# Three stages of a four-layer conv network: merged gates and moved projections in a state-space scan, re-ordered passes in an edge stage, four buffers and two queues for the norm statistics

## The reference, cut to what matters

```python
def _gn(v, G=16, eps=1e-5):
    B_, C_, H_, W_ = v.shape
    g = v.reshape(B_, G, C_ // G, H_, W_)
    m = jnp.mean(g, axis=(2, 3, 4), keepdims=True)
    s = jnp.var(g, axis=(2, 3, 4), keepdims=True)
    return ((g - m) / jnp.sqrt(s + eps)).reshape(v.shape)
...
x = x + L0(_gn(x)); x = x + L1(_gn(x)); x = x + L2(_gn(x)); x = x + L3(x's edge operators and an hourglass)
```

```python
xi, z = jnp.split(xz_, 2, axis=-1)
xi = jax.nn.silu(causal_dwconv1d(xi.transpose(0, 2, 1), conv1d_w, conv1d_b)).transpose(0, 2, 1)
x_dbl = xi @ x_proj_w.T
dt = jax.nn.softplus(x_dbl[..., :DT_RANK] @ dt_proj_w.T + dt_proj_b)
Bm = x_dbl[..., DT_RANK:DT_RANK + D_STATE]
Cm = x_dbl[..., DT_RANK + D_STATE:]
dA = jnp.exp(dt[..., None] * A); dBu = dt[..., None] * Bm[:, :, None, :] * u[..., None]   # in selective_scan
h = scan of h = dA * h + dBu along the sequence
y = jnp.einsum('bldn,bln->bld', h, Cm) + u * D          # u is xi
return y * jax.nn.silu(z)                               # then out_proj
```

## Time and profile before

| | us |
|---|---|
| median of 3 runs | 18979.34 (18858.6 to 18991.37) |
| the profiled run, its own time | 18992.29 |
| span of that run in the trace | 18990.6 |

### The profile page before, as it was taken

One profiled execution on the slowest core, in us unless ns is written; L12 is line 12 of the kernel. 1 busy time (PEld: TensorE's weight loads), 2 busy tenths in 40 slices (PEclk: granted clock), 3 DMA queues, 4 the chain that ended last, 5 costly groups with the idle time before them and its releaser, 6 DMA issues. The chain is left out here.

```text
span 18990.6 us, 422049 instructions
## 1 busy us (share of the span) xinstructions
PE 15091.1 (79%) x162396; PEld 5743.9 (30%) x162396; DVE 14262.7 (75%) x12961; ACT 12928.0 (68%) x20898; POOL 9582.0 (50%) x8230
## 2 busy tenths in 40 slices
PE   5888888888885668888888888848888886658877
PEld 2333333333332312222222222212222222435554
...
GB/s 80 12 11 12 11 12 11 12 11 12 11 12 103 112 53 16 17 17 17 17 17 17 17 17 17 15 100 32 43 35 37 42 33 59 166 48 32 32 46 132
DMA packets 773987, 711.83 MB, mean 37 GB/s; under 512 B 260672, under 2 KB 671456, under 8 KB 753384
## 3 DMA queue, kind: packets, MB, share of 16 engines
q1 hardware_dynamic: 691736, 584.15, 11.8%
...
...
## 5 line engine op out<-in xcount | busy, mean ns | idle before, releaser
L270 DVE TENSOR_TENSOR l_mx<-l_p_v,l_puN 128x2048 f32<-128x2048 f32 x2560 | 5636.4, 2278 | 154.9 <-PE l_p_s L485 142.2
L485 PE MATMUL l_p_s<-l_mx,l_w2z 128*32 128x512 f32 x32768 | 3825.9, 611 | 588.7 <-ACT l_mx L397 319.6
L290 POOL TENSOR_TENSOR l_mx<-l_pv,l_puP 128x2048 f32<-128x2048 f32 x1024 | 3716.7, 3646 | 319.3 <-PE l_p_s L485 313.5
L1270 POOL TENSOR_TENSOR l1m_hc<-l1m_hs,l1m_cs 128x512 f32<-128x512 f32 x2304 | 2929.1, 1271 | 8.5 <-DVE l1m_hs L1222 8.1
L1222 DVE TENSOR_TENSOR_SCAN l1m_hs<-l1m_da,l1m_carry,l1m_pu 128x512 f32<-128x512 f32 x2304 | 2823.5, 1267 | 106.2 <-ACT l1m_da L1140 2.2
L416 ACT ACTIVATE l_mx<-l_pv,l_puP 128x128 f32<-128x128 f32 x8192 | 2446.9, 393 | 0.8
L1212 DVE TENSOR_TENSOR l1m_pu<-l1m_pu,l1m_bs 128x512 f32<-128x512 f32 x2304 | 1475.8, 686 | 1102.2 <-PE l1m_pu L975 1102.2
L397 ACT ACTIVATE l_mx<-l_mx 128x2048 f32<-128x2048 f32 x1024 | 1954.5, 1909 | 46.3 <-POOL l_mx L290 46.0
L485 PEld LDWEIGHTS l_p_s<-l_mx,l_w2z 128*32 128x32 f32 x32768 | 983.4, 112 | 3029.3 <-issue 1770.0
L1140 ACT ACTIVATE l1m_da<-l1m_pr,l1m_an 128x512 f32<-128x512 f32 x2304 | 1459.0, 684 | 565.3 <-PE l1m_pr L968 414.6
L975 PE MATMUL l1m_pu<-l1m_dts,l1m_sl 32*128 32x512 f32 x4608 | 1415.9, 690 | 480.4 <-ACT l1m_da L1140 470.7
...
## 6 DMA issues: line engine op xcount, KB each, us to landing
...
l_xs<-in_x_dram SPq DMA_DIRECT2D x128, 256.0 KB, 3.0
x_after<-l_ot SPq DMA_DIRECT2D x128, 256.0 KB, 2.4
...
```

The costliest lines, as they stand in the source:

```text
L270: v.tensor_tensor(mx[:, r % QB, :, :, :], columns.unsqueeze(1).broadcast_to([P, 4, G, P]), rows.broadcast_to([P, 4, G, P]), ALU.max).then_ ...
L290: g.tensor_tensor(mx[:, r % QB, :, :, :], pv[:, u, :, :].unsqueeze(1).broadcast_to([P, 4, G, P]), rows.broadcast_to([P, 4, G, P]), ALU.add ...
L485: ins = pe.matmul(p_s[R * q:R * (q + 1), 512 * u:512 * (u + 1)], w2z[:, 31 - r:63 - r], mx[:, r % QB, q, :, :].rearrange("p t v -> p (t v) ...
L1270: g.tensor_tensor(hc[:, (3 * u + p) % 6, part, :], hs[:, p % 3, part, :], cs[:, u, :], ALU.mult).then_inc(hc_done, 1)
```

## The change

**norm_table.** `xt` has four buffers. The even images are loaded by SP, the odd ones by ACT's queue; a load of image n waits until the statistics of image n-4 are done. The loops are unrolled.

**state_space.** The uses of `pp` stand in the order X0, X1, DT0, DT1, BB, CC, Z0, Z1, OUT. ACT no longer applies Silu to PSUM: drain_x (p = 0, 1) and drain_z (p = 7, 8) write a half into a new SBUF tile `raw`, and both gates are applied in p = 2, two halves in one instruction each (gate_x for chunk n, gate_z for chunk i), with a table load before and an explicit one behind. The matmuls follow the drains: x_proj(n,1) at p = 1, z_proj at p = 7 and 8. dt_proj waits for gate_x, POOL's gate for gate_z. DVE's multiplication of a pair is one instruction over two banks, and the skip of the chunk behind stands ahead of pair 2's multiplication.

**edges.** POOL clears the whole of `xs` in one memset (14256 columns) in place of its four borders; the gathers stand ahead of passes(0); in the loop weigh(b+1) is first and all seven early passes of image b+2 follow pool(b,0). `sides` and `rim` are rewritten, with the same matmuls in the same order.

```diff
-        xt = m.sb("xt", [P, 2, N])
+        xt = m.sb("xt", [P, 4, N])
...
-                    sp.wait_ge(s_free, j * 2 + u + 1)
-                    sp.dma_start(xt[:, u, :], image[at(j * 2 + u), :, :].rearrange("b p n -> p (b n)")).then_inc(s_load[u], 16)
+            for n in range(0, B, 2):
+                if n >= 4:
+                    sp.wait_ge(s_free, n - 1)
+                sp.dma_start(xt[:, n % 4, :], image[n]).then_inc(s_load[n % 4], 16)
...
         @block.scalar
         def _(act):
+            for n in range(1, B, 2):
+                if n >= 4:
+                    act.wait_ge(s_free, n - 1)
+                act.dma_start(xt[:, n % 4, :], image[n]).then_inc(s_load[n % 4], 16)
...
-    X0, Z0, X1, Z1, DT0, DT1, BB, CC, OUT = range(USES)
+    X0, X1, DT0, DT1, BB, CC, Z0, Z1, OUT = range(USES)
...
             def dt_proj(n, un, ho):
+                pe.wait_ge(xi_ready, n + 1)
                 into_pp(n, (DT0, DT1)[ho])
...
                     if p == 1 and not last:
-                        z_proj(n, un, 0)
-                    if p == 2 and not last:
                         x_proj(n, un, 1)
-                        z_proj(n, un, 1)
...
+                        if p == 7:
+                            z_proj(n, un, 0)
+                        if p == 8:
+                            z_proj(n, un, 1)
                     if p == 8:
                         out_proj(i, use_of(N, 0) if last else use_of(n, OUT))
...
-                act.activation(xi[:, un, hf, :], pp[:, :], ACT.Silu, bias=cols[:, 0, hf:hf + 1]).then_inc(pp_drained, 1)
+                act.activation(raw[:, 0, hf, :], pp[:, :], ACT.Identity, bias=cols[:, 0, hf:hf + 1]).then_inc(pp_drained, 1)
...
-                act.activation(sz[:, un, hf, :], pp[:, :], ACT.Silu).then_inc(pp_drained, 1)
+                act.activation(raw[:, 1, hf, :], pp[:, :], ACT.Copy).then_inc(pp_drained, uses)
+
+            def gate_x(n, un, ahead):
+
+                act.wait_ge(pp_drained, use_of(n, X1) + 1)
+                if ahead:
+                    act.wait_ge(y1_done, n * 2)
+                act.activation(xi[:, un], raw[:, 0], ACT.Silu).then_inc(xi_ready, 1)
+
+            def gate_z(i, u):
+
+                act.wait_ge(pp_drained, use_of(i, Z1) + 1)
+                act.wait_ge(y2_done, i * 2 + 1)
+                act.activation(sz[:, u], raw[:, 1], ACT.Silu).then_inc(sz_ready, 1)
...
+                    if p == 2:
+                        if not last:
+                            a_of(n, un, jn)
+                            gate_x(n, un, True)
+                        gate_z(i, u)
+                        act.preload_act_table_set("natural_log_exp_and_others")
                     if not last:
                         if p == 0:
-                            gate_x(n, un, 0, True)
+                            drain_x(n, 0, True)
                         if p == 1:
-                            gate_z(n, un, 0, True)
-                        if p == 2:
-                            a_of(n, un, jn)
-                            gate_x(n, un, 1, True)
-                            gate_z(n, un, 1, True)
+                            drain_x(n, 1, True)
...
+                        if p == 7:
+                            drain_z(n, 0, True)
+                        if p == 8:
+                            drain_z(n, 1, True)
                     if p == 8:
                         out_copy(j, u, use_of(N, 0) if last else use_of(n, OUT))
...
-                for part in range(2):
-                    bank = 2 * ((u + p) % 2) + part
-                    tile = pu[:, LC * bank:LC * (bank + 1)]
-                    dve.tensor_tensor(tile, tile, bs[:, u, :], ALU.mult).then_inc(dbu_done, 1)
+                bank = 2 * ((u + p) % 2)
+                tile = pu[:, LC * bank:LC * (bank + 2)].rearrange("p (a n) -> p a n", a=2)
+                dve.tensor_tensor(tile, tile, bs[:, u, :].unsqueeze(1).broadcast_to([NB, 2, LC]), ALU.mult).then_inc(dbu_done, 2)
...
                 for p in range(PAIRS):
+                    if p == 2:
+                        skip(i - 1, 1 - u, 1, i * D_IN + (8 + 4))
                     inputs_by_b(i, u, p)
                     scans(i, u, p)
-                    if p == 2:
-                        skip(i - 1, 1 - u, 1, i * D_IN + (8 + 4))
...
-            g.memset(xs[:, :, :, 0:2], 0.0)
-            g.memset(xs[:, :, :, W + 2:W + 4], 0.0)
-            g.memset(xs[:, :, 0:2, 2:W + 2], 0.0)
-            g.memset(xs[:, :, XR - 2:XR, 2:W + 2], 0.0).then_inc(zeroed, 1)
+            g.memset(xs[:], 0.0).then_inc(zeroed, 1)
...
             for b in range(B):
-                if b + 2 < B:
-                    passes(b + 2, 0, 2)
                 if b + 1 < B:
                     weigh(b + 1)
                 pool(b, 0)
                 if b + 2 < B:
-                    passes(b + 2, 2, 7)
+                    passes(b + 2, 0, 7)
```

204 lines of the change are left out of this document (99 added, 105 removed).

## The result

The changed kernel took 18184.19 us (median of 4, 18156.89 to 18191.61), the kernel before 18918.97 beside it: a ratio of 0.9609, with an interval from 0.956 to 0.9657. The forecast was 18050, its wide range 17850 to 18430, the likeliest case's own range 17960 to 18200. The profiled run spans 18189.9 us against 18990.6, 800.7 less; the forecast gain was 935.

A forecast was written before the change was run, and what follows sets the result against it. The prediction took DVE, with holes in it, to bound the state-space stage. From 18992 it subtracted 755 (state space), 64 (statistics) and 116 (edges), giving 18057, predicted as 18050; likeliest range 17960 to 18200, wide range 17850 to 18430.

The forecast's parts named there:

- the likeliest case: Whole kernel: state-space chunk near 37.6 us, time 18050 us, own range 17960 to 18200, chance 0.44.
- the wait at pair 5: State-space stage: DVE loses 1.0 us at full clock or 1.9 at 1.2 GHz, behind both loads and gates.
- most of it at pair 5: State-space sign of being right: DVE waits about 3 us per chunk, mostly at pair 5 and ahead of the skip.
- The cover of the edge stage: Edge stage: the 16.23 us wait ahead of pool(b,1) has room for the two moved passes, 9.3 us.
- the first step of the chain: State-space chunk: replicate(0) starts about 2.2 us after DVE's first multiplication, behind the second z_proj and out_proj's drain.
- a sign of being wrong: State-space stage: replicate(0) starting later than 2.2 us into the chunk would show the prediction wrong.
- The rest of the chain: State-space chunk after replicate(0): PE and ACT steps bring replicate(4) at 19.6 us; later projections are covered by DVE's pairs.
- 0.8 for the skip: State-space stage: DVE loses about 0.8 us per chunk where the skip, now ahead of pair 2, waits for the reduces.
- the merging's 0.05 per pair: State-space stage: one 1024-column multiplication takes 1.22 us, not 1.27 for two, giving a pair pitch of 3.68.
- The clock: State-space stage: PE's idle time brings 1.2 GHz, so pair 5 loses 1.9 us, not 1.0, and the pair behind 0.4.
- the clock holds: State-space rival: full clock in PE's gap, chunk 36.3 us, another 150 us gained, total 17900; chance 0.18.
- the prediction's own terms: Statistics: DVE's waits fall from 102.1 to 26 + 7 + 2 = 35 us, a gain of about 64 us.

The follow-up runs named there:

- the faster one: Changed kernel plus late reduces, further steps out of PE's loop, one-queue statistics and old edge start: 17858.48 us; with the skip moved inside pair 3, 17867.08 us.

## Why the prediction was right, and where a term was off

**What held.** Table loads fell from eight to two per chunk; the load is followed by its activation without a gap (30.01 + 1.28, then 31.31), so it costs its own 1.28 us and no more, as the earlier trace rows had it. The multiplication took 1.218 us. Both loads and gates stand between two decays, and the wait at pair 5 is what was forecast (0.89 to 1.98; forecast 1.0 to 1.9). DVE's wait ahead of the multiplication is 2.73 us, forecast about 3, but "most of it at pair 5" did not hold: pair 5 has 1.31 of it, pairs 1 and 7 have 1.42. The granted clock falls in PE's gap and is back by pair 6. The cover of the edge stage held: PE waits 4.5 us per image, forecast 3 to 6, and 6.6 us are left ahead of pool(b,1); `weigh` came 14.1 us later at its start, forecast 14, of which the stage felt 11.

**The term that was mis-sized** is the first step of the chain: "replicate(0) starts at about 2.2". It started at 3.28, which the prediction had named as a sign of being wrong. From the start of out_proj to that of replicate(0) are 1.87 us, so the forecast let out_proj start some 0.3 us into the chunk; it started at 1.41, since replicate(8), the second z_proj, ACT's decays and the drain follow each other without slack. These 1.1 us are as much as the difference between 37.6 and 38.7: 1.1 x 128 = 141 us, the 141 that the stage is short of. The rest of the chain nearly cancels: from replicate(0) to replicate(4) the chunk shown took 17.63 us, forecast 17.4, and from there to the next chunk's pair 0 17.64, forecast 18.0. That the step is the cause is worked out so; no run gave out_proj its early start back by itself. By the order of the streams the change itself put that wait there, moving the second z_proj directly ahead of out_proj on a bank that only ACT can free.

**What was right by luck.** I added DVE's waits as if each had its own price (0.8 for the skip, 1.9 for pair 5, 0.4 behind it, and the merging's 0.05 per pair). The runs show that a change of DVE's own work has none: moving the skip is worth 0 within 20 us in the changed kernel and in the faster one, and so is the merged multiplication in the changed kernel. The sum came out near because DVE's waits and work fill the chunk by definition, and the chain that I had followed to place them was the true bound. Had I closed that chain round the chunk, from one replicate(0) to the next, it would have asked for no price of DVE's waits at all.

**The clock** was put at 0.9 + 0.4 us per chunk and is 0.5; the rival "the clock holds" would have given 60 us, not 150.

**The statistics** won 55 us, not 64 (the prediction's own terms make 102.1 - 35 = 67). The pace was better than forecast (4.76 per image, DVE's own work, with no wait), the start worse: image 0 landed at 19.0, 9.3 us later than before and not 2.4, since SP's queue got almost nothing moved while ACT's image 1 was under way. The Trainium skill, "DMA: Bandwidth & Descriptors", Specifications, puts the HBM limit of a core at some 358 GB/s, half of a stack's 716. The stretch above, on a core that ran alone, moved 437, and the measurement decides. The same page, Issuing engines are not separate DMA queues, says that transfers started by several engines run on the same 16 DMA engines and interleave, and that a second issuer saves issue time alone. The two runs in which queues and buffers were parted agree on the rate: the second queue brought none (111.1 us of waits against 102.1). On the interleaving the traces agree only later: from 9 to 18 us the two queues of the changed kernel moved 2.11 and 1.77 MB, but from 2 to 8 us 0.06 and 2.11.

Open is why two chunks that follow each other differ at the low clock (pair 5 waits 0.89 in one and 1.98 in the next): the clock comes back before replicate(4) in 51 chunks and after it has begun in 26, and no run here tells why. Open is also why the first 8 us of the statistics go to ACT's queue. How the stage's gain divides between the fewer table loads and the moved projections was not tried apart.
